# Attention and expert layer on one core: weighed sums in pairs, sums of squares from two fp32r halves, the key's projection in two steps, bounds read earlier

## Chip, cores, metric

One core of one Trainium2 chip. The metric is the device time of one execution in microseconds (us), the median of several runs.

## The reference, cut to what is computed

```python
# x: (4, 512, 512), context: (4, 512, 512), 32 heads of 16, D = 512
def xattn(x, context, Wq, Wk, Wv):
    q = x @ Wq.T; k_raw = context @ Wk.T; v_raw = context @ Wv.T
    q = q.reshape(b, n, 32, 16).transpose(0, 2, 1, 3)
    kv = jnp.concatenate([k_raw, v_raw], axis=-1).reshape(b, m, 32, 16, 2)
    k = kv[..., 0].transpose(0, 2, 1, 3); v = kv[..., 1].transpose(0, 2, 1, 3)
    q, k = rmsnorm(q), rmsnorm(k)            # over the 16 of a head
    attn = softmax(einsum('bhnd,bhmd->bhnm', q, k) * 16 ** -0.5)
    return einsum('bhnm,bhmd->bhnd', attn, v)...

x = x + xattn(layernorm(x), ctx, Wq, Wk, Wv)
# then a layer of 7 routed experts (top 2 of 7) and one shared expert, each
#   u = t @ Wup + bup;  g = silu(u @ Wgate + bgate) * u;  y = g @ Wdown + bdown
x = x + ffn(layernorm(x))
```

## The kernel before

The kernel has two phases. **Attention** takes the first 452 us or so. It runs over 16 units: unit u is one batch b of four and one group g of four, a group being 128 of the 512 columns, that is 8 heads. Each unit has eight steps s; a step is one half of the heads (`ab`, s // 4) against 128 of the 512 keys (`mt`, s % 4). "Step 6" below always means s = 6 of a unit. Projections are made two units ahead: while unit u is in its steps, TensorE makes the queries of unit u + 2 into PSUM bank `bank_b` (`q_turns`) and its keys into `bank_a` (`k_turns`). One such projection is 12 matmuls of 128x128 by 512 columns, called turns. Everything there is fp32 split in a high and a low fp32r part, three products for one.

What each engine does for a step, in its own program order (each engine waits on semaphores; nothing else sets the order):

- TensorE: `scored(u, s)` writes the scores into the PSUM tile `scores` (8 matmuls on 32 rows each). There is one such tile, so it waits until the exponential of the step before has been taken. Then `between(u, s)`: some turns, sums, transposes. Then `weighed(t - 1)`: the probabilities of the step before by the values (`o_ps`, 4 fp32 matmuls on 17 columns each, recorded as 8). Then `after(u, s)`.
- ScalarE: `before_exp(u, s)`, a small operation or two (squares, logarithm, root, copy of `o_ps`), then the exponential of `scores` into `probs`, of which there are two.
- VectorE: `step(u, s)`, a list of normalisations, splits and copies out of PSUM.
- GpSimd: two squarings of roots for each unit, and now and then a layer norm (`norm2`).

The sum over each head's 16 squares for the rms norm goes like this: ScalarE squares the projection out of its bank into the SBUF tile `sq`, TensorE multiplies `sq` by a matrix of ones in blocks (`blocks`) in plain fp32 into the PSUM tile `tr` (`sum_q`, `sum_k`), VectorE takes `tr` (`sums_q`, `sums_k`), ScalarE takes the root. `tr` is used in turn by many things, in a fixed order, the transposes of the outputs (`out_transposes`, L708) and the routing (`gate_parts`, `gates`, `norm2_transposes`) among them. In unit u, `square_q(u + 2)` stands ahead of the exponential of step 6 and `sum_q(u + 2)` in step 7; `square_k(u + 1)` stands ahead of that of step 2 and `sum_k(u + 1)` in step 2.

Units are not alike. With g = 1 of the first three batches VectorE also splits the next batch's input in step 6 (`x_low`, `x_split`), with g = 2 it splits the next context in steps 1 to 3 (`context_split`), and with g = 2 and g = 3 of the first three batches TensorE makes the next values too (`v_all`, 12 matmuls in step 2 and 12 in step 5). For the last two units nothing is projected.

**Experts** take the rest: the shared expert on 8 tiles of 256 rows (`tile(0)` to `tile(7)`), then the routed experts on tiles whose number is only known at run time. During tiles 2 to 6 the routing is worked out: `starts` gives where each expert's tiles begin, `table_out` which rows stand in which slot. From it GpSimd gathers the rows of the first routed tile (`gather(NA)`), which TensorE transposes within tile 7. The engines read the expert bounds into registers (`bound`).

Of the kernel before, what the change touches and what calls it, by code (L numbers as in the profile page):

```python
# [15 lines left out]
def moe_layer(nc, x, x_t, ctx_t, wq_t, wk_t, wv_t, w_all, b_up_gate, b_down, w_router, b_router, gate_bias, xn_dram,  # L16
# [20 lines left out]
    with ExitStack() as ctx:  # L37
# [46 lines left out]
        probs = asb("probs", [P, 2, QUADS, SEQ])  # L84
# [95 lines left out]
        K_TURNS = {6: (0, 4), 7: (4, 5), 0: (5, 9), 1: (9, 12)}  # L180
        Q_TURNS = {3: (0, 5), 4: (5, 9), 5: (9, 12)}
# [142 lines left out]
        def _(pool):  # L324
# [8 lines left out]
            def root(n, half):  # L333
# [11 lines left out]
                                    pattern=[[HD, P // HD], [0, HD]], channel_multiplier=-1).then_inc(blocks_set, 1)  # L345
            nc.gpsimd.memset(v_sb[0][:, :, :, HD:], 1.0).then_inc(ones_set, 1)
# [50 lines left out]
            def gather(n):  # L397

                first = isinstance(n, int) and n == NA
                if first:  # L400
                    pool.wait_ge(xl_done, n * 2)
                    pool.wait_ge(table_ready, 1)
                    pool.wait_ge(dense_stored, 16)
# [201 lines left out]
        def _(pe):  # L605
# [8 lines left out]
            def scored(u, s):  # L614
# [16 lines left out]
            def weighed(t):  # L631
# [149 lines left out]
            def between(u, s):  # L781
# [1237 lines left out]
```

## Time and profile before

| | |
|---|---|
| median of 3 runs | 966.19 us (966.05 to 966.67) |
| the profiled execution, time | 966.36 us |
| the profiled execution, span | 964.6 us |
| TensorE busy | 944.2 us (98%) |
| VectorE busy | 706.1 us (73%) |
| ScalarE busy | 497.4 us (52%) |
| GpSimd busy | 208.1 us (22%) |

The span is what the trace covers. The time is that of the same execution as the runs are timed, 1.8 us above its span. Busy time of TensorE counts an operation until its modelled end, so that two short waits between overlapping operations hardly show in it.

### The profile page before, as it was taken

How to read it: one execution, taken by the hardware profiler on the slowest of the kernel's cores; microseconds unless marked ns; L12 is line 12 of the kernel's file. 1: busy time of each engine (PE TensorE's matmuls, PEld its weight loads, DVE VectorE, ACT ScalarE, POOL GpSimd, SP SyncE). 2: the span in 40 equal slices, each digit the busy share in tenths (PEclk: the TensorE clock that was granted, in tenths of full speed). 3: DMA queues.
4: the chain of work that ended last, by engine and by line, in shares of the span. 5: the costliest groups of instructions: out<-in, count | busy, mean ns of one | idle time of the engine just before them, and what ended most of it. 6: DMA issues, size and time to landing. Idle time of an engine off the chain costs nothing.

```text
span 964.6 us, 17835 instructions
## 1 busy us (share of the span) xinstructions
PE 944.2 (98%) x6676; PEld 681.4 (71%) x6676; DVE 706.1 (73%) x1459; ACT 497.4 (52%) x619; POOL 208.1 (22%) x225
## 2 busy tenths in 40 slices
PE   8999999999999999999999999999999999999995
PEld 7634444454444454345989999999999999999995
DVE  7798767886678757885978886865867686758654
ACT  4588668866787658887234313323424244324221
POOL 1011000311012200320300001423323323333331
PEclk9999999999999999999999999999999999999998
DMA  9400100100201110313523104834535536625422
GB/s 334 170 1 23 66 1 1 45 33 24 76 2 44 45 66 1 110 56 130 203 74 112 67 23 142 235 73 71 180 67 146 117 71 204 197 48 166 115 49 39
DMA packets 32512, 87.42 MB, mean 91 GB/s; under 512 B 7744, under 2 KB 7744, under 8 KB 28352
## 3 DMA queue, kind: packets, MB, share of 16 engines
q1 hardware_dynamic: 21920, 60.70, 17.9%
q0 software_dynamic: 10528, 25.87, 12.9%
q8 instruction: 40, 0.66, 0.3%
q14 instruction: 24, 0.20, 0.1%
HBM read 61.83 MB, written 24.72 MB: 90 GB/s over the span
## 4 chain that ended last, share of the span: by engine, by line
PE 87%; DVE 6%; issue 2%; ACT 2%; DMA 1%; DVEq 0%; POOLq 0%; POOL 0%; SPq 0%; ACTq 0%
PE z_ps L907 16%; PE y_ps L907 15%; PE u_ps L907 15%; PE o_ps L642 11%; PE scores L626 8%; PE bank_a L679 5%; PE bank_b L663 5%; PE bank_b L649 2%; PE xt_ps L921 2%; PE bank_a L649 2%; PE tr L708 1%; PE tr L702 1%; PE tr L697 1%; DMA ctx_raw<-ctx_t 1%; ACT probs L1180 1%
## 5 line engine op out<-in xcount | busy, mean ns | idle before, releaser
L1180 ACT ACTIVATE probs<-scores 128x2048 f32<-128x2048 f32 x128 | 240.5, 1879 | 64.1 <-PE scores L626 61.1
L907 PE MATMUL z_ps<-u_hi,w_sb 128*128 128x256 f32 x896 | 167.6, 285 | 0.8 <-DVE u_lo L1869 0.8
L907 PE MATMUL u_ps<-x_hi,w_sb 128*128 128x256 f32 x864 | 159.2, 283 | 0.0
L1210 ACT ACTIVATE u_hi<-u_ps,b_ug 128x256 fp32r<-128x256 f32 x108 | 45.3, 471 | 198.8 <-PE u_ps L907 198.8
L907 PEld LDWEIGHTS z_ps<-u_hi,w_sb 128*128 128x128 f32 x896 | 140.6, 190 | 2.1 <-DVE u_lo L1869 1.2
L907 PE MATMUL y_ps<-w_sb,g_hi 128*128 128x512 f32 x448 | 139.8, 393 | 0.2 <-DVE g_lo L1887 0.2
L907 PEld LDWEIGHTS u_ps<-x_hi,w_sb 128*128 128x128 f32 x864 | 135.7, 190 | 1.1
L642 PE MATMUL o_ps<-probs,v_sb 128*17 128x512 f32 x1024 | 134.7, 598 | 0.0
L907 PE MATMUL z_ps<-u_lo,w_sb 128*128 128x256 f32 x448 | 126.5, 282 | 0.0
L907 PE MATMUL u_ps<-x_lo,w_sb 128*128 128x256 f32 x432 | 122.2, 283 | 0.0
L1222 ACT ACTIVATE s_sb<-z_ps,b_ug 128x256 f32<-128x256 f32 x112 | 47.0, 471 | 99.6 <-PE z_ps L907 99.6
L626 PEld LDWEIGHTS scores<-q_st,k_hi 32*128 32x128 f32 x512 | 24.7, 182 | 104.0 <-ACT probs L1180 63.4
L427 POOL DMA_INDIRECT out<-y_sb,target x42 | 67.3, 1602 | 127.8 <-DVEq L1911 120.4
L907 PEld LDWEIGHTS y_ps<-w_sb,g_hi 128*128 128x128 f32 x448 | 82.3, 188 | 17.2 <-issue 0.8
L1869 DVE SCALAR_TENSOR_TENSOR u_lo<-u_ps,b_ug,u_hi 128x256 fp32r<-128x256 f32 x108 | 47.2, 478 | 64.0 <-ACT u_hi L1210 61.5
L907 PE MATMUL y_ps<-w_sb,g_lo 128*128 128x512 f32 x224 | 88.0, 393 | 0.0
L907 PEld LDWEIGHTS z_ps<-u_lo,w_sb 128*128 128x128 f32 x448 | 85.1, 190 | 0.0
L907 PEld LDWEIGHTS u_ps<-x_lo,w_sb 128*128 128x128 f32 x432 | 82.2, 190 | 1.1
L1882 DVE SCALAR_TENSOR_TENSOR g_sb<-u_ps,b_ug,s_sb 128x256 f32<-128x256 f32 x112 | 53.9, 481 | 30.3 <-ACT s_sb L1222 30.1
L626 PE MATMUL scores<-q_st,k_hi 32*128 32x512 f32 x512 | 64.7, 494 | 3.5 <-ACT probs L1180 1.9
L350 POOL TENSOR_TENSOR r<-r 128x512 f32<-128x512 f32 x16 | 17.4, 1088 | 189.5 <-ACT r L1067 189.5
L1190 ACT ACTIVATE w_sb<-w_raw 128x1024 fp32r<-128x1024 f32 x42 | 42.3, 1058 | 28.1 <-PE y_ps L907 28.1
(247 smaller groups left out, 1594.9 us busy)
## 6 DMA issues: line engine op xcount, KB each, us to landing
w_raw<-w_all SPq DMA_DIRECT2D x27, 1024.0 KB, 6.9
ctx_raw<-ctx_t SPq DMA_DIRECT2D x4, 1024.0 KB, 6.8
out<-x_sb SPq DMA_DIRECT2D x16, 256.0 KB, 2.0
xg<-xt_dram POOLq DMA_DIRECT2D x14, 256.0 KB, 3.4
x_sb<-x SPq DMA_DIRECT2D x1, 3072.0 KB, 17.4
xn<-x_t SPq DMA_DIRECT2D x12, 256.0 KB, 4.4
xn_dram<-xn SPq DMA_DIRECT2D x12, 256.0 KB, 2.1
xt_dram<-xt SPq DMA_DIRECT2D x6, 512.0 KB, 3.0
```

The costliest lines, as they stand in the source:

```text
L427: nc.gpsimd.indirect_dma_start(out=out, in_=y_sb[:, h, :], in_offset=None, compute_op=ALU.add, out_offset=bass.IndirectOffsetOnAxis(ap=tar ...
L626: last = nc.tensor.matmul(scores[:, j, :], part[rows, u % 2, ab, mt * P:(mt + 1) * P], q_st[rows, u % 2, ab, :], start=(part is k_hi), sto ...
L642: last = nc.tensor.matmul(o_ps[32 * j:32 * j + HD + 1, :], v_sb[b % 2][:, mt, head, :], probs[:, t % 2, j, :], start=(mt == 0), stop=(mt = ...
L663: last = nc.tensor.matmul(bank_b[:], (wq_hi, wq_lo)[a][:, g, c, :], (xt_hi, xt_lo)[b][:, c, :], start=(c == 0 and a + b == 0), stop=(c == ...
L679: last = nc.tensor.matmul(bank_a[:], (wk_hi, wk_lo)[a][:, g, c, :], (ctx_hi, ctx_lo)[b][:, c, :], start=(c == 0 and a + b == 0), stop=(c = ...
L907: ins = nc.tensor.matmul(out_ps, stat[a], mov[b], start=(first and a + b == 0), stop=(last and a == 1), skip_group_check=True)
L1180: nc.scalar.activation(probs[:, t % 2], scores[:], ACT.Exp).then_inc(p_ready, 1)
L1190: nc.scalar.activation(w_sb[par][:, m, 0, two], w_raw[:, m, two], ACT.Copy).then_inc(hi_done, 1)
L1210: last = nc.scalar.activation(u_hi[:, c, :], u_ps[:, b, a, :], ACT.Identity, bias=b_ug[:, par, 0, c:c + 1])
L1222: nc.scalar.activation(s_sb[:, c, :], z_ps[:, b, a, :], ACT.Silu, bias=b_ug[:, par, 1, c:c + 1]).then_inc(s_done, 1)
L1869: nc.vector.scalar_tensor_tensor(u_lo[:, c, :], u_ps[:, b, a, :], bias[:, c:c + 1], u_hi[:, c, :].bitcast(FP32), ALU.add, ALU.subtract)\
L1882: nc.vector.scalar_tensor_tensor(g_sb[:, c, :], u_ps[:, b, a, :], bias[:, c:c + 1], s_sb[:, c, :], ALU.add, ALU.mult).then_inc(g_done, 1)
```

## The change

- **Weighed sums.** `probs` has three buffers. In units 0 to 13 `weighed` comes straight behind `scored` (in steps 2 and 7 behind `between`), and by the table `SUMMED` in these steps: 0 (those of steps 6 and 7 of the unit before), 2 (step 0), 3 (steps 1 and 2), 4 (step 3), 6 (steps 4 and 5), none in 1, 5 and 7.
- **Squares.** For 20 of the sums (`HALVED`: the 14 `sum_q(u + 2)` and the `sum_k(u + 1)` of the six units with g of 2 or 3 in the first three batches) GpSimd copies `sq` into the fp32r tile `sq_hi` (`squares_high`), VectorE writes the rest `sq_lo` (`squares_low`), and TensorE sums the two in two fp32r matmuls in place of one fp32 matmul (`sum_halves`). VectorE's piece stands in step 6 behind `stack_k`, or in step 2.
- **Turns.** `k_turns(u + 2)` has 6 turns in step 7 and 6 in step 1 of the next unit, behind `sum_q`; it had 4, 1, 4 and 3 in steps 6, 7, 0 and 1. `q_turns` has 1, 5 and 6 turns in steps 3, 4 and 5; it had 5, 4 and 3.
- **Buffers.** `q_st`, `k_hi` and `k_lo` have one copy in place of two, so that their writers wait for `scored` of the unit before (`half_scored`).
- **Experts.** VectorE reads the bounds in pieces in tiles 4 to 7 ahead of the gate's products (`during_z`), not all at the end of tile 7. The first gather takes its rows straight from `table`, not from a copy in `index`, and GpSimd reads its bound ahead of it.

```diff
-        probs = asb("probs", [P, 2, QUADS, SEQ])
+        probs = asb("probs", [P, 3, QUADS, SEQ])
-        q_st = asb("q_st", [P, 2, 2, SEQ], FP32R)
-        k_hi, k_lo = (asb(n, [P, 2, 2, CTX], FP32R) for n in ("k_hi", "k_lo"))
+        q_st = asb("q_st", [P, 2, SEQ], FP32R)
+        k_hi, k_lo = (asb(n, [P, 2, CTX], FP32R) for n in ("k_hi", "k_lo"))
...
-        K_TURNS = {6: (0, 4), 7: (4, 5), 0: (5, 9), 1: (9, 12)}
-        Q_TURNS = {3: (0, 5), 4: (5, 9), 5: (9, 12)}
+        K_TURNS = {7: (0, 6), 0: (6, 6), 1: (6, 12)}
+        Q_TURNS = {3: (0, 1), 4: (1, 6), 5: (6, 12)}
+        SUMMED = {0: (-2, -1), 1: (), 2: (0,), 3: (1, 2), 4: (3,), 5: (), 6: (4, 5), 7: ()}
...
+            def squares_high(use):
+                pool.wait_ge(sqk_done if use[0] == "sum_k" else sqq_done, use[1] + 1)
+                for other, n in HALVED.items():
+                    if n == HALVED[use] - 1:
+                        pool.wait_ge(tr_ready, TR_AT[other] + 1)
+                nc.gpsimd.tensor_copy(sq_hi[:], sq[:]).then_inc(sq_high, 1)
...
+            def sum_halves():
+                nc.tensor.matmul(tr[:], blocks_r[:], sq_hi[:], start=True, stop=False)
+                nc.tensor.matmul(tr[:], blocks_r[:], sq_lo[:], start=False, stop=True).then_inc(tr_ready, 1)
+
             def sum_q(u):
                 begin("tr", TR_AT, ("sum_q", u), tr_free)
-                pe.wait_ge(sqq_done, u + 1)
-                nc.tensor.matmul(tr[:], blocks[:], sq[:], start=True, stop=True).then_inc(tr_ready, 1)
+                if ("sum_q", u) in HALVED:
+                    pe.wait_ge(sq_low, HALVED["sum_q", u] + 1)
+                    sum_halves()
...
                 elif s == 7:
                     if ahead:
+                        sum_q(u + 2)
                         k_turns(u + 2, *K_TURNS[s])
-                    if ahead:
-                        sum_q(u + 2)
...
             for u in range(UNITS):
                 for s in range(STEPS):
                     scored(u, s)
-                    between(u, s)
-                    if u or s:
-                        weighed(STEPS * u + s - 1)
+                    alone = u >= UNITS - 2
+                    if alone or s in (2, 7):
+                        between(u, s)
+                    for back in SUMMED[s] if not alone or (u, s) == (UNITS - 2, 0) else (s - 1,):
+                        if u or back >= 0:
+                            weighed(STEPS * u + back)
+                    if not alone and s not in (2, 7):
+                        between(u, s)
                     after(u, s)
...
+            def squares_low(use):
+                dve.wait_ge(sq_high, HALVED[use] + 1)
+                nc.vector.tensor_tensor(sq_lo[:], sq[:], sq_hi[:].bitcast(FP32), ALU.subtract).then_inc(sq_low, 1)
...
                     if nxt:
                         stack_k(u + 1, 0)
+                    if u + 2 < UNITS:
+                        squares_low(("sum_q", u + 2))
...
-            gather(NA)
             pool.wait_ge(start_ready, 1)
             total = bound(pool, ER)
+            gather(NA)
             gather(NA + 1)
...
-            tile(7, 0, x_tile=14, during_u=last_split, during_y=bounds)
+            tile(7, 0, x_tile=14, during_u=last_split, during_z=lambda: bounds(7, ER + 1))
```

How the change moves instructions, at the places that the prediction speaks of. TensorE of unit 8, step 7 and step 0 of unit 9 before (`bank_a` rows are turns of `k_turns`, the `sq,blocks` row is `sum_q(10)`):

```order
L626 MATMUL scores<-q_st,k_hi 128x512 x4
L626 MATMUL scores<-q_st,k_lo 128x512 x4
L679 MATMUL bank_a<-ctx_lo,wk_hi 128x512
L697 MATMUL tr<-sq,blocks 128x512
L642 MATMUL o_ps<-probs,v_sb 17x512 x4
L626 MATMUL scores<-q_st,k_hi 128x512 x4
L626 MATMUL scores<-q_st,k_lo 128x512 x4
L679 MATMUL bank_a<-ctx_hi,wk_lo 128x512
L679 MATMUL bank_a<-ctx_hi,wk_hi 128x512
L679 MATMUL bank_a<-ctx_lo,wk_hi 128x512
L679 MATMUL bank_a<-ctx_hi,wk_lo 128x512
L642 MATMUL o_ps<-probs,v_sb 17x512 x4
```

The same steps of TensorE now, from step 7 on:

```order
L660 MATMUL scores<-q_st,k_hi 128x512 x4
L660 MATMUL scores<-q_st,k_lo 128x512 x4
L729 MATMUL tr<-sq_hi,blocks_r 128x512
L730 MATMUL tr<-sq_lo,blocks_r 128x512
L713 MATMUL bank_a<-ctx_hi,wk_hi 128x512
L713 MATMUL bank_a<-ctx_lo,wk_hi 128x512
L713 MATMUL bank_a<-ctx_hi,wk_lo 128x512
L713 MATMUL bank_a<-ctx_hi,wk_hi 128x512
L713 MATMUL bank_a<-ctx_lo,wk_hi 128x512
L713 MATMUL bank_a<-ctx_hi,wk_lo 128x512
L660 MATMUL scores<-q_st,k_hi 128x512 x4
L660 MATMUL scores<-q_st,k_lo 128x512 x4
```

The sum stands first behind the scores of step 7, with six turns behind it and no weighed sum in that step.

VectorE of unit 5 (g = 1) now, from the transposes' copy of step 5 (`rec`, `o_n`, `x_sb` are `finalize`) to `sums_q` of step 7 (`ssq`):

```order
L1512 RECIPROCAL rec<-tr 128x16
L1513 TENSOR_TENSOR o_n<-tr,rec 128x256
L1518 TENSOR_TENSOR x_sb<-x_sb,o_n 128x4x4x16
L1394 TENSOR_TENSOR xt_lo<-xn,xt_hi 128x512
L1400 CAST xt_hi<-xn 128x512
L1401 TENSOR_TENSOR xt_lo<-xn,xt_hi 128x512
L1501 STREAM_SHUFFLE twin<-kn 128x512
L1504 TENSOR_SCALAR k_hi<-twin,sign 128x512
L1505 SCALAR_TENSOR_TENSOR k_lo<-twin,sign,k_hi 128x512
L1441 TENSOR_TENSOR sq_lo<-sq,sq_hi 128x512
L1445 TENSOR_TENSOR ssq<-tr,eps 128x512
```

The row `sq_lo` is new, ahead of `ssq`; the others stand as before. In units with g = 0 the three rows of `xt_lo` and `xt_hi` are missing.

GpSimd around the first gather, before:

```order
L407 COPY index<-table 128x2
L411 DMA xg<-xn_dram,index 128x520 x2
L293 TENSOR_LOAD start_i
L293 ISA x2
L407 COPY index<-table 128x2
```

and now:

```order
L312 TENSOR_LOAD start_i
L312 ISA x2
L446 DMA xg<-xn_dram,table 128x520 x2
L441 COPY index<-table 128x2
L446 DMA xg<-xn_dram,index 128x520 x2
```

The copy ahead of the first gather is gone, and the read of the bound stands ahead of it.

## Rows read from the trace of the kernel before

**Rows 1.** The page: busy time by engine (part 1), costliest groups (part 5).
```profile
PE 944.2 (98%) x6676; PEld 681.4 (71%) x6676; DVE 706.1 (73%) x1459; ACT 497.4 (52%) x619; POOL 208.1 (22%) x225
...
L642 PE MATMUL o_ps<-probs,v_sb 128*17 128x512 f32 x1024 | 134.7, 598 | 0.0
```

**Rows 2.** TensorE's waits, 30 to 455 us: total, times, longest, in us.
```profile
PE scores L626 <- ACT probs L1180: 1.9, 4, 0.7
```

**Rows 3.** Timeline of unit 8 from step 5: start, duration, engine.
```profile
267.46 0.50 PE L626 MATMUL scores<-q_st,k_hi 32*128 32x512 f32 x4
...
268.92 0.60 PE L708 MATMUL tr<-ident,o_sb 128*128 128x128 f32 x4
...
270.03 0.59 ACT L1038 ACTIVATE sq<-bank_b 128x512 f32<-128x512 f32 x1
270.44 0.50 PE L626 MATMUL scores<-q_st,k_hi 32*128 32x512 f32 x4
...
272.23 1.05 PE L642 MATMUL o_ps<-probs,v_sb 128*17 128x512 f32 x8
...
272.94 0.68 DVE L1290 BATCH_NORM_STATS2 stats<-x_sb 128x6 f32<-128x512 f32 x1
273.21 0.51 PE L626 MATMUL scores<-q_st,k_hi 32*128 32x512 f32 x4
...
274.22 1.02 PE L697 MATMUL tr<-sq,blocks 128*128 128x512 f32 x2
...
276.16 0.50 PE L626 MATMUL scores<-q_st,k_hi 32*128 32x512 f32 x4
```

**Rows 4.** Timeline: starts of steps 2 and 3 of unit 9.
```profile
282.01 0.51 PE L626 MATMUL scores<-q_st,k_hi 32*128 32x512 f32 x4
...
284.73 0.50 PE L626 MATMUL scores<-q_st,k_hi 32*128 32x512 f32 x4
```

**Rows 5.** Timeline: step 5 of unit 9, VectorE's last piece ahead, unit 10.
```profile
290.51 0.50 PE L626 MATMUL scores<-q_st,k_hi 32*128 32x512 f32 x4
...
297.48 0.75 DVE L1438 SCALAR_TENSOR_TENSOR k_lo<-twin,sign,k_hi 128x512 fp32r<-128x512 f32 x1
...
299.23 0.51 PE L626 MATMUL scores<-q_st,k_hi 32*128 32x512 f32 x4
```

**Rows 6.** Timeline of unit 10 (g = 2), from the start of step 1 to step 3.
```profile
302.89 0.51 PE L626 MATMUL scores<-q_st,k_hi 32*128 32x512 f32 x4
...
304.23 1.10 POOL L350 TENSOR_TENSOR r<-r 128x512 f32<-128x512 f32 x1 [9.14 <-ACT r L1067]
...
304.47 1.41 DVE L1430 SCALAR_TENSOR_TENSOR q_st<-twin,lower,q_st 128x512 fp32r<-128x512 f32 x1
...
309.25 0.69 DVE L1321 TENSOR_TENSOR ctx_lo<-ctx_raw,ctx_hi 128x512 fp32r<-128x512 f32 x1
...
311.43 0.51 PE L626 MATMUL scores<-q_st,k_hi 32*128 32x512 f32 x4
```

**Rows 7.** Timeline: GpSimd's layer norm in unit 7.
```profile
222.60 2.35 POOL L366 TENSOR_SCALAR xn<-x_sb,mv,rsqrt 128x512 f32<-128x512 f32 x1 [12.10 <-PE tr L747]
```

**Rows 8.** Timeline: starts of units 11 and 12.
```profile
330.69 0.51 PE L626 MATMUL scores<-q_st,k_hi 32*128 32x512 f32 x4
...
361.66 0.51 PE L626 MATMUL scores<-q_st,k_hi 32*128 32x512 f32 x4
```

**Rows 9.** TensorE's waits, 560 to 680 us, in us.
```profile
PE xt_ps L921 <- DMA xg<-xn_dram,index: 0.7, 1, 0.7
PE z_ps L907 <- DVE u_lo L1869: 0.6, 1, 0.6
```

**Rows 10.** Timeline: GpSimd's first gather; VectorE's first copy of tile 7.
```profile
575.27 0.91 POOL L407 COPY index<-table 128x2 int32<-128x2 int32 x1 [22.89 <-DVE table L1858]
...
577.08 1.12 POOL L411 DMA_INDIRECT xg<-xn_dram,index  x1 [0.90 <-POOL index L407]
...
597.58 0.69 DVE L1903 TENSOR_TENSOR y_sb<-y_ps,bd 128x512 f32<-128x512 f32 x1 [4.21 <-issue]
```

More of the change, by code:

```diff
@@ L177, in moe_layer @@
         A_AT, B_AT, TR_AT = uses("a"), uses("b"), uses("tr")
-        K_TURNS = {6: (0, 4), 7: (4, 5), 0: (5, 9), 1: (9, 12)}
-        Q_TURNS = {3: (0, 5), 4: (5, 9), 5: (9, 12)}
+        SUMS = [("sum_k", 0), ("sum_q", 0), ("sum_q", 1)]
+        HALVED = {}
+        for u in range(UNITS):
+            _, g, more, _ = batch_of(u)
+            if u + 1 < UNITS:
+                SUMS.append(("sum_k", u + 1))
+                if more and g >= 2:
+                    HALVED[SUMS[-1]] = len(HALVED)
+            if u + 2 < UNITS:
+                SUMS.append(("sum_q", u + 2))
+                HALVED[SUMS[-1]] = len(HALVED)
+        K_TURNS = {7: (0, 6), 0: (6, 6), 1: (6, 12)}
+        Q_TURNS = {3: (0, 1), 4: (1, 6), 5: (6, 12)}
+        SUMMED = {0: (-2, -1), 1: (), 2: (0,), 3: (1, 2), 4: (3,), 5: (), 6: (4, 5), 7: ()}
         def tile_of(b, i):
@@ L382, in _ @@
                     norm2(b - 1, 2)
+                if u + 2 < UNITS:
+                    squares_high(("sum_q", u + 2))
+                if behind and g == 2:
                     norm2(b - 1, 3)
@@ L625, in scored @@
                         rows = slice(32 * j, 32 * j + 32)
-                        last = nc.tensor.matmul(scores[:, j, :], part[rows, u % 2, ab, mt * P:(mt + 1) * P],
-                                                q_st[rows, u % 2, ab, :], start=(part is k_hi), stop=(part is k_lo),
+                        last = nc.tensor.matmul(scores[:, j, :], part[rows, ab, mt * P:(mt + 1) * P],
+                                                q_st[rows, ab, :], start=(part is k_hi), stop=(part is k_lo),
                                                 skip_group_check=True)
@@ L1033, in x_high, with squares_taken @@
                 nc.scalar.activation(xt_hi[:, c, :], xn[:, c % 2 if b else c, :], ACT.Copy).then_inc(xt_high, 1)
+            def squares_taken(use):
+                ahead = SUMS[SUMS.index(use) - 1]
+                if ahead in HALVED:
+                    act.wait_ge(sq_low, HALVED[ahead] + 1)
+                else:
+                    act.wait_ge(tr_ready, TR_AT[ahead] + 1)
             def square_q(u):
                 act.wait_ge(b_ready, B_AT["q", u] + 1)
-                act.wait_ge(tr_ready, TR_AT["sum_k", max(u - 1, 0)] + 1 if u != 1 else TR_AT["sum_q", 0] + 1)
+                squares_taken(("sum_q", u))
                 nc.scalar.activation(sq[:], bank_b[:], ACT.Square).then_inc(sqq_done, 1)
@@ L1042, in square_k @@
                 if u:
-                    act.wait_ge(tr_ready, TR_AT["sum_q", u] + 1)
+                    squares_taken(("sum_k", u))
                 nc.scalar.activation(sq[:], bank_a[:], ACT.Square).then_inc(sqk_done, 1)
@@ L1561, in step @@
                         context_split(b + 1, 1)
+                    if ("sum_k", u + 1) in HALVED:
+                        squares_low(("sum_k", u + 1))
                     if u == 0:
@@ L1935, in _, with bounds @@
             tile(3, 0, x_tile=6, before_x=totals_out, during_z=probabilities, during_y=steps_of(prefixes_out, starts))
-            tile(4, 0, x_tile=8, during_u=positions, during_y=lambda: hot_rows(0))
-            tile(5, 0, x_tile=10, during_u=lambda: hot_cols(0),
+            start_at = [0]
+            def bounds(first, end):
+                dve.wait_ge(start_ready, 1)
+                for e in range(first, end):
+                    start_at.append(bound(dve, e))
+            tile(4, 0, x_tile=8, during_u=positions, during_z=lambda: bounds(1, 3), during_y=lambda: hot_rows(0))
+            tile(5, 0, x_tile=10, during_u=lambda: hot_cols(0), during_z=lambda: bounds(3, 5),
                  during_y=steps_of(lambda: table_out(0), lambda: hot_rows(1)))
```

66 lines of the change are left out of this document (39 added, 27 removed).

## Prediction

> **What bounds the kernel now.** The page comes first: TensorE is busy 98% of the span, the weighed sums alone 134.7 us [rows 1]. Then the waits of TensorE in attention: in all of it only 1.9 us for the exponential [rows 2]. So attention is bound by TensorE's program, and what counts is each step's length, from one start of `scored` to the next. The timeline of one unit gives it, with its parts. Step 7 of unit 8 puts one turn between `scored` and the sum, 1.01 us after the step's start; step 5 puts three there, 1.46 us. So a turn is 0.23 us. Step 6 has four turns and reaches its weighed sum after 1.79 us, one turn and one change of shape (0.11 us) more than step 5; `scored` is then 0.67 us. A weighed sum takes 0.98 us to the next step (272.23 to 273.21), the fp32 sum 0.96 us (274.22, a weighed sum and 276.16), the transposes of step 5 0.54 us [rows 3]. Below all this lies a floor: `scores` is one tile, so a step is never shorter than scores, exponential and hand-over. Step 2 of unit 9 shows it, 2.72 us [rows 4]. Step 6 of unit 8 at 2.77 us is hardly above.
>
> Two stretches outside attention wait: 0.7 us for the first gathered rows and 0.6 us for `u_lo` [rows 9].
>
> **The change on TensorE alone.** Two weighed sums in a row should cost 0.98 + 0.86 us: each of the two passes of one streams for 0.43 us, since the group's mean is 598 ns and the pair spans 1.05 us [rows 1, 3], and only the last has a drain behind it. Bounds for the second are 0.86 and 0.98; I take 0.86. The halved sum takes two turns, 0.46 for 0.96 us. With these, a unit with g = 0 goes: step 0 with two weighed sums 2.5, so the floor 2.72; step 1 waits for ScalarE, which copies `o_ps` and takes a root after the second weighed sum, 2.87 (an estimate; together with step 0 5.59 us, against 282.01 - 276.16 = 5.85 now [rows 3, 4]); step 2 the floor; step 3 0.67 + 1.84 + 0.44 = 2.95; step 4 0.67 + 0.98 + 1.36 = 3.01; step 5 0.67 + 1.48 + 0.54 = 2.69, so the floor; step 6 the floor; step 7 0.67 + 0.46 + 1.37 + changes 0.2 = 2.70, so the floor. Sum 22.43 us against 23.07 of unit 9 [rows 3, 5]. So where nothing is late, 0.6 us a unit is all that is left of the saving, since the floor takes the rest.
>
> **The sum is late.** `sum_q` now stands first in step 7 and needs GpSimd's copy and VectorE's rest. Everything in units counts from the start of step 5 (T5).
>
> - The transposes of step 5 now stand behind six turns: T5 + 0.67 + 1.48 = 2.15 us, not 1.46 [rows 3]. VectorE's program has `finalize`, `stack_k` and then `squares_low`. In unit 8 VectorE is through with `stack_k` 4.02 us after the transposes start (268.92 to 272.94), waiting for nothing but these [rows 3]. So `squares_low` begins at 6.17, takes 0.69 as a subtraction of this shape does [rows 6], and with 0.1 for the hand-over the sum starts at 6.96.
> - TensorE is there at T5 + 2.72 + 2.72 + 0.67 = 6.11. It waits 0.85 us with six turns and the next `scored` queued behind. From the sum to the next unit are eight turns and two changes, 2.03: T5 + 8.99, so steps 5 to 7 take 9.0 us where they took 8.70 [rows 3]. With the other steps the unit is 23.3, +0.2. Units 4, 8, 12 and 13: **+0.9**.
> - GpSimd's copy: the square is taken 0.41 us before step 6 [rows 3], so the copy runs from T5 + 3.2. The trace has no such copy. It costs nothing at the price of the nearest row, 1.10 [rows 6], done at 4.3; at 2.35, the layer norm's [rows 7], done at 5.6, still ahead of 6.17. I take 1.1.
> - g = 1 with input to split: VectorE starts `k_lo` 6.97 us after T5 and needs 0.7 more before it could go on [rows 5]. The transposes' later place adds 0.2. So `squares_low` begins at 7.85, the sum at 8.63, the next unit at T5 + 10.66, against 8.72 [rows 5]. The steps before give 0.1 back. Units 5 and 9: +1.9 each. Unit 1 has a first step that now waits less: +1.2. In unit 0 VectorE is held up by the weights' splits just as far: +2.0. Together **+6.9**.
> - g = 2: `sum_k` is halved too, and stands behind `v_even` in step 2. VectorE starts the `ctx_lo` ahead of it 6.36 us after the start of step 1 [rows 6]. The rows for the next batch's epsilon had a weighed sum behind them in step 0 and have none now, so that VectorE's chain from them falls 0.98 us later in step 1. `squares_low` begins at 6.36 + 0.63 + 0.98 = 7.97, or at 7.3 without the hold of 0.66 us on `q_st` (below). TensorE could sum at 2.72 + 0.67 + 0.98 + twelve turns with a change, 2.87 = 7.24. Steps 1 and 2 together come to 8.7 to 9.4; I take 9.0, against 8.54 [rows 6]. In steps 6 and 7 VectorE has `v_out`, `stack_k`, the new piece and `parts_out` ahead of the sum: a wait of some 0.6 us. Against this step 0 gains 0.2 and step 5 0.3, and step 4 loses 0.3. Unit 10, 31.46 us now [rows 5, 8], goes to 32.0; units 2, 6 and 10: **+1.4**.
> - g = 3: here the copies have room in step 2. Step 0 saves 0.5 to 0.7, step 1 0.35, step 2 0.4, step 5 0.3; step 4 loses 0.2 and the last two steps 0.1. Unit 11 goes from 30.97 [rows 8] to 29.6; units 3, 7 and 11: **-3.3**.
> - Unit 14 keeps its weighed sums single but has six turns in step 1 where it had three, with a change for 0.6 us less the floor's 0.05 in step 0: **+0.5**. The third buffer of `probs` and the single buffers of `q_st` and `k_hi` cost nothing: their writers come a step or more after the last reader.
>
> Attention: +0.9 + 6.9 + 1.4 - 3.3 + 0.5 = **+6.4 us**.
>
> **Experts.** The gather starts where the copy does now, at 575.27 and not at 577.08 [rows 10]: 1.8 us earlier against a wait of 0.7 [rows 9], which goes. VectorE stands 4.21 us before its first copy of tile 7 reading seven bounds [rows 10], 0.6 each; now two at most stand in a tile's z phase, ahead of products with about that much slack. Then `u_lo` is in time and 0.6 goes [rows 9]. **-1.3 us**; if the two reads delay a `g_lo`, -1.0.
>
> Sum: 966.36 us, the profiled execution, + 6.4 - 1.3 = 971.5; the median lies 0.2 below that execution, so **971.3 us**.
>
> **A lock between VectorE and GpSimd.** In unit 10 `q_st`, two SBUF inputs, takes 1.41 us where it starts 0.24 us into GpSimd's squaring of 1.10 us [rows 6]; the one of this form ahead of the sum in unit 9 takes 0.75 [rows 5]. So it seems to have stood until GpSimd was done. The new copy would run from T5 + 3.2 in units with g = 0, where VectorE's `x_sb` addition (two SBUF inputs) is due at 3.7: 0.5 us more in the chain to the sum. The same in g = 1 (0.4) and ahead of `sum_k` in g = 2 (0.3): about +4 us, and 975.5 us in all. The Trainium skill ("SBUF — State Buffer", section "SBUF: two separate sides") states it as a rule: such an operation and one of GpSimd that reads SBUF hold the shared port pair exclusively, and the second fully blocks. By that rule the answer is this rival's 975.5, without it 971.3. The trace agrees in unit 10.
>
> **Rivals.**
> 1. *The sum is late as worked out*, 971.3 us. For it: the program order and unit 8's chain, in which VectorE waits for nothing else. Own range 967 to 974. Chance 0.45.
> 2. *Late, and the lock too*: 975.5. Against it: a GpSimd copy may be shorter than 1.1 us. Chance 0.17.
> 3. *Gain and loss cancel*: the sum comes 0.3 us earlier at each of its 17 late places (14 in step 7, 3 in step 2), 971.3 - 5.1 = 966.2. For it: my chains rest on the old order. Chance 0.18.
> 4. *Faster: the sum is not late*. Then all waits go: 2.3 in unit 0, 2.2 in units 1, 5 and 9, 0.85 in four units, about 0.6 in the six with g of 2 and 3, and 1.1 in three steps 2: 19 us, and 952 us. It decides if VectorE reaches `squares_low` by T5 + 5.3; unit 8's row has it at 5.48 even with the old, earlier transposes (272.94 - 267.46). So only part of it can come: with half of it 962. Chance 0.20.
>
> **How the numbers follow.** The measurement tells 0.2%, 1.9 us, from no change. Below 964.3: rival 4 and a part of rival 3, 0.23. Within: most of rival 3 and the lower edge of rival 1, 0.17. Above 968.1: 0.60. The range is 962 to 977: it leaves out the better half of rival 4 and a lock that costs more than reckoned.
>
> **What would show it.** TensorE's waits would have `tr <- sq_lo` as by far the longest, 14 to 20 times, 15 to 20 us in total, the longest over 2 us in units 0, 1, 5 and 9. Step 7 of a g = 0 unit would be about 3.5 us, step 3 2.95 and step 0 2.72; two weighed sums 1.84 us to the next instruction. Both waits of rows 9 would be gone. The prediction is wrong if `sq_lo` waits are under 5 us in total, if step 3 is over 3.1 us (the second weighed sum drains), or if GpSimd's copy and not VectorE ends the wait.

## The result: 977.2 us, a little slower

| | before | after |
|---|---|---|
| median | 966.29 us (966.05 to 966.67, 4 runs) | 977.2 us (976.19 to 978.18, 4 runs) |
| profiled execution, time / span | 966.36 / 964.6 us | 976.19 / 974.4 us |
| start of step 7 of unit 15 (attention all but over) | 451.62 us | 463.43 us |
| mean granted TensorE clock | 0.996 | 0.991 |

The ratio is 1.0112, with a 95% interval of 1.0099 to 1.0125. So the kernel is slower, as forecast, but the time lies just above the forecast range. The spans differ by 9.8 us: attention takes 11.8 us more, and what comes after it 2.0 us less (974.4 - 463.43 = 510.97 against 512.98). The four runs of after lie in two pairs, 976.2 and 976.3 with a recorded mean clock of 0.991 and 0.990, and 978.1 and 978.2 with 0.989 both; the profile is of the first.

**The page after.** TensorE's busy time and the chain that ended last:

```profile
PE 932.4 (96%) x6676; PEld 690.0 (71%) x6676; DVE 719.5 (74%) x1479; ACT 495.7 (51%) x619; POOL 220.8 (23%) x245
PE 81%; DVE 10%; ACT 4%; issue 3%; POOLq 0%; POOL 0%; DVEq 0%; ACTq 0%
```

TensorE has less to do, 932.4 against 944.2 us, and still ends later; VectorE has a tenth of the chain. Its waits in attention, 30 to 470 us (us in total, times, longest), where before there were [rows 2], 1.1 us once for `q_st` and 0.5 us more:

```profile
PE tr L729 <- DVE sq_lo L1441: 15.3, 10, 2.8
PE scores L660 <- ACT probs L1236: 3.7, 9, 1.3
PE tr L729 <- DVE xn L1420: 2.1, 4, 0.5
PE bank_b L683 <- DVE qn L1457: 1.8, 3, 0.6
```

In the experts the waits of [rows 9] are both gone.

**A unit with g = 0.** The timeline of unit 8 from step 5, which answers to [rows 3]:

```profile
275.38 0.50 PE L660 MATMUL scores<-q_st,k_hi 32*128 32x512 f32 x4
...
277.55 0.60 PE L754 MATMUL tr<-ident,o_sb 128*128 128x128 f32 x4
...
278.60 0.61 POOL L385 CAST sq_hi<-sq 128x512 fp32r<-128x512 f32 x1 [4.87 <-ACT sq L1094]
...
280.82 0.51 PE L660 MATMUL scores<-q_st,k_hi 32*128 32x512 f32 x4
...
281.56 0.69 DVE L1441 TENSOR_TENSOR sq_lo<-sq,sq_hi 128x512 fp32r<-128x512 f32 x1
...
282.40 0.47 PE L729 MATMUL tr<-sq_hi,blocks_r 128*128 128x512 f32 x1 [0.83 <-DVE sq_lo L1441]
...
284.40 0.50 PE L660 MATMUL scores<-q_st,k_hi 32*128 32x512 f32 x4
```

`squares_low` starts 6.18 us after the step 5 it is counted from, the sum at 7.02, the next unit at 9.02. The forecast had 6.17, 6.96 and 8.99. GpSimd's copy takes 0.61 us, and is done 2.3 us before anyone needs it.

**A unit with g = 1.** The timeline of unit 9, steps 6 and 7 and the start of unit 10, which answers to [rows 5]:

```profile
298.33 4.82 POOL L395 TENSOR_SCALAR xn<-x_sb,mv,rsqrt 128x512 f32<-128x512 f32 x2
...
302.94 0.69 DVE L1394 TENSOR_TENSOR xt_lo<-xn,xt_hi 128x512 fp32r<-128x512 f32 x1
303.10 1.00 POOL L385 CAST sq_hi<-sq 128x512 fp32r<-128x512 f32 x1
303.55 0.83 DVE L1400 CAST xt_hi<-xn 128x512 fp32r<-128x512 f32 x1
304.23 0.50 PE L660 MATMUL scores<-q_st,k_hi 32*128 32x512 f32 x4 [0.19 <-ACT probs L1236]
...
306.98 0.68 DVE L1441 TENSOR_TENSOR sq_lo<-sq,sq_hi 128x512 fp32r<-128x512 f32 x1
307.81 0.47 PE L729 MATMUL tr<-sq_hi,blocks_r 128*128 128x512 f32 x1 [2.85 <-DVE sq_lo L1441]
...
309.31 0.63 PE L713 MATMUL bank_a<-ctx_lo,wk_hi 128*128 128x512 f32 x1
...
310.29 0.80 PE L660 MATMUL scores<-q_st,k_hi 32*128 32x512 f32 x4
```

Here two things stand that no term of the forecast had. While GpSimd copies, a CAST of VectorE takes 0.83 us, where the same one took 0.42 before the change. And some 1.4 us behind the end of the wait of 2.85 us TensorE turns slow: the first turns behind the sum take 0.39 us as ever, from 309.31 on they take 0.63, and `scored`'s first four matmuls 0.80 and not 0.50. The table of stretches around the four long waits (columns: us, busy time of PE, PEld, DVE, ACT, POOL with the number of instructions, granted clock, DMA share, GB/s) has unit 0's wait and slow stretch, unit 1's slow stretch, unit 5's wait and what follows it, and unit 9's wait with three stretches behind it:

```profile
60.00:62.50 2.50, 0.00 (x0) 0.00 (x0) 2.43 (x5) 1.88 (x1) 0.00 (x0) 1.00 0.00 0
63.40:66.90 3.50, 3.50 (x18) 1.75 (x20) 3.12 (x7) 0.81 (x2) 0.00 (x0) 0.51 0.03 7
90.70:94.20 3.50, 3.50 (x19) 1.11 (x21) 3.01 (x6) 1.91 (x2) 0.00 (x0) 0.51 0.00 0
195.30:198.10 2.80, 0.04 (x4) 0.00 (x0) 2.64 (x6) 1.88 (x1) 0.00 (x0) 1.00 0.57 179
198.10:202.00 3.90, 3.84 (x28) 2.09 (x32) 2.74 (x6) 1.66 (x2) 0.00 (x0) 1.00 0.02 4
304.90:307.80 2.90, 0.06 (x4) 0.02 (x1) 2.69 (x6) 1.88 (x1) 0.00 (x0) 1.00 0.55 171
307.80:309.20 1.40, 1.39 (x6) 1.19 (x7) 0.66 (x1) 0.00 (x0) 0.00 (x0) 1.00 0.00 0
309.20:312.60 3.40, 3.40 (x19) 1.19 (x22) 3.02 (x7) 1.66 (x2) 0.00 (x0) 0.50 0.02 5
312.60:314.90 2.30, 2.30 (x20) 1.07 (x12) 0.03 (x1) 1.76 (x3) 0.00 (x0) 1.00 0.00 0
```

The granted clock has two levels, 1.2 and 2.4 GHz, so that 0.50 is the lower one throughout. It is down for 3.4 us each time, from 0.9 to 1.5 us after TensorE is back at work: behind the waits of unit 0 (2.57 us), unit 1 (2.70) and unit 9 (2.85). Behind that of unit 5, 2.82 us, it isn't down at all. The Trainium skill ("TensorE: Matmul & The Clock Gate", section "Part 1: The HAM clock gate (the "warmup" mystery)") says that the array's clock is halved after a stretch without work and comes back after sustained work; the rows agree for units 0, 1 and 9, and unit 5 shows that a stand of the same length doesn't always bring it.

### The profile page after: what moved, and what is told of

Its sections match the earlier page's. It is cut to its first block, busy times and chain, and to the rows that moved or that the text cites. A ratio compares the mean times of both kernels' runs of the same rounds, so it can differ in the third digit from the quotient of the medians.

```text
span 974.4 us, 17952 instructions
## 1 busy us (share of the span) xinstructions
PE 932.4 (96%) x6676; PEld 690.0 (71%) x6676; DVE 719.5 (74%) x1479; ACT 495.7 (51%) x619; POOL 220.8 (23%) x245
## 4 chain that ended last, share of the span: by engine, by line
PE 81%; DVE 10%; ACT 4%; issue 3%; POOLq 0%; POOL 0%; DVEq 0%; ACTq 0%
PE y_ps L955 16%; PE z_ps L955 16%; PE u_ps L955 16%; PE o_ps L676 8%; PE scores L660 6%; PE bank_b L697 4%; ACT probs L1236 3%; PE bank_a L713 3%; PE bank_b L683 2%; PE xt_ps L969 2%; PE bank_a L683 2%; DVE twin L1501 1%; PE tr L748 1%; DVE k_lo L1505 1%; DVE sq_lo L1441 1%
## 5 line engine op out<-in xcount | busy, mean ns | idle before, releaser
L676 PE MATMUL o_ps<-probs,v_sb 128*17 128x512 f32 x1024 | 127.9, 601 | 0.0
L676 PEld LDWEIGHTS o_ps<-probs,v_sb 128*17 128x17 f32 x1024 | 21.7, 97 | 60.0 <-issue 59.0
```

## The experiments

All but e4 start from the changed kernel. Times are medians, with the ratio to before and its interval.

**e1: all sums whole again, in fp32.** All else as changed (pairs of weighed sums, turns, experts):

```diff
+        HALVED = {}
-                if u + 2 < UNITS:
+                if ("sum_q", u + 2) in HALVED:
                     squares_high(("sum_q", u + 2))
```
(the same condition ahead of `squares_low` in VectorE's step 6)

> The changed kernel with all sums of squares in one fp32 matmul straight from sq again; pairs, turns, buffers and the experts' part stay. Theory A (the halves are late and TensorE stands for them, and loses its clock behind the longest of these stands): no wait for sq_lo is left, step 7 of a unit with g = 0 is about 3.2 us and not 3.57, that of units 1, 5 and 9 3.2 and not 5.6 to 6.1, the granted clock is 1.00 throughout attention; some 14 us less than the changed kernel, 962 to 964 us. Rival B (the pairs and the turns' new places are what costs): it stays near 976 us.

Measured: **960.37 us**, ratio 0.9937 (0.9921 to 0.9954). The time is 2 us below the range of theory A, and rival B falls. The waits for `sq_lo` are gone, and step 7 is 3.11 us in all units with g of 0 and 1. So the split of the squares alone turns a gain of 6 us into a loss of 11. Without it nearly every kind of unit is shorter than before: 22.9 against 23.07 (g = 0, unit 8), 31.03 against 31.46 (unit 10), 29.50 against 30.97 (unit 11).

**e2: the low half first.** `squares_low` is VectorE's first piece of step 6, ahead of the splits and `stack_k`:

```diff
+                    if u + 2 < UNITS:
+                        squares_low(("sum_q", u + 2))
                     if nxt:
                         stack_k(u + 1, 0)
-                    if u + 2 < UNITS:
-                        squares_low(("sum_q", u + 2))
```

> The changed kernel with VectorE's squares_low of sum_q first in step 6, ahead of x_low and stack_k, and not behind them. Theory A (VectorE's queue is what makes the sum late): step 7 of a unit with g = 0 falls from 3.57 to 2.75 us, that of units 1, 5 and 9 to 2.8 to 3.0; with g of 2 and 3 behind a first batch parts_out still holds the bank tr, so that these keep 3.65; 957 to 959 us in all. Rival (GpSimd's copy is the late link): VectorE waits for sq_high instead and step 7 stays over 3.3 us, above 970 us.

Measured: **963.92 us**, ratio 0.9973 (0.9963 to 0.9983), 5 to 7 us short of what was expected. In g = 0 it does what it should: unit 8 takes 22.61 us, step 7 2.82. In units 1, 5 and 9 step 7 still takes 3.60, 4.06 and 4.03 us. TensorE's waits:

```profile
PE scores L660 <- ACT probs L1236: 6.9, 13, 1.5
PE scores L660 <- DVE k_lo L1505: 3.4, 3, 1.3
...
PE tr L729 <- DVE sq_lo L1441: 0.6, 1, 0.6
```

and why, in unit 9:

```profile
289.36 4.82 POOL L395 TENSOR_SCALAR xn<-x_sb,mv,rsqrt 128x512 f32<-128x512 f32 x2
294.14 0.60 POOL L385 CAST sq_hi<-sq 128x512 fp32r<-128x512 f32 x1
294.85 0.69 DVE L1441 TENSOR_TENSOR sq_lo<-sq,sq_hi 128x512 fp32r<-128x512 f32 x1 [0.90 <-POOL sq_hi L385]
...
299.29 0.51 PE L660 MATMUL scores<-q_st,k_hi 32*128 32x512 f32 x4 [1.26 <-DVE k_lo L1505]
```

GpSimd's copy stands behind two layer norms in its own queue. VectorE now waits 0.90 us for it with the splits and `stack_k` queued behind, and 0.90 + 0.69 later it is `k_lo` that is late: `scored` of unit 10 waits 1.26 us. So in units 5 and 9 the rival's condition, VectorE waiting for `sq_high`, did hold. The wait moved from `tr` to `scores`. By these numbers VectorE has about 0.3 us of room there (0.90 + 0.69 - 1.26) for a piece of 0.69, so that `k_lo` would be late even without the wait for GpSimd; this is an estimate, the copy ahead of the layer norms was not tried. In unit 1, with no such wait, `scored` still waits 0.84 us for `k_lo`.

**e3: TensorE kept at work in the long waits.** Ten matmuls of 128 columns, whose result nobody reads, ahead of the sum in units 0, 1, 5 and 9:

```diff
                     if ahead:
+                        if u in (0, 1, 5, 9):
+                            pe.wait_ge(a_free, A_AT["k", u + 2])
+                            unread(bank_a[:, 0:P], 10)
                         sum_q(u + 2)
```

> The changed kernel with ten matmuls of 128x128 that nobody reads (some 2.3 us) in step 7 of units 0, 1, 5 and 9 ahead of the sum that TensorE waits for. They do no needed work and are done before the sum could start. If the drop of the granted clock behind these waits costs what I read from the steps behind them (scored at 1.15 and not 0.67 us), the clock is 1.00 there, steps 7 and 0 of these units lose 0.4 to 1.1 us each, and the time is some 4 to 6 us less than the changed kernel, 971 to 973 us. If the clock is not the reason for the slow steps, it is unchanged or some tenths slower.

Measured: **972.07 us**, ratio 1.0057 (1.0040 to 1.0074), 5.1 us below the changed kernel's median (4.1 by the spans of the two profiled executions), and the mean clock is 0.996 again. The stretches at and behind unit 9's sum now have the full clock:

```profile
305.00:307.40 2.40, 2.03 (x12) 1.45 (x12) 1.24 (x4) 0.40 (x1) 0.00 (x0) 1.00 0.00 1
307.40:312.00 4.60, 4.60 (x43) 2.23 (x43) 3.46 (x8) 3.44 (x5) 0.78 (x1) 1.00 0.00 0
```

The sums are no earlier. The gains stand in units 0 (32.71 to 31.79), 1 (26.19 to 25.32), 2 (31.64 to 30.55), 9 (25.89 to 25.41) and 10 (32.63 to 31.52), that is at and behind the sums of units 0, 1 and 9. Unit 5, where the changed kernel had kept its clock, stays as it was (25.39, 25.43), and unit 6 too: nothing but the held clock shows in the times. Steps 7 and 0 around each of the three slow stretches are together 1.4 to 1.5 us shorter.

**e4: the experts' part alone**, on the kernel before: the first gather reads `table` itself, and the bounds are read in tiles 4 to 7.

```diff
-                nc.gpsimd.tensor_copy(index[:], table[:, bass.ds((n - NA + 1) * 2, 2)]).then_inc(index_ready, 1)
+                    picked_rows = table[:, 2:4]
...
-            tile(7, 0, x_tile=14, during_u=last_split, during_y=bounds)
+            tile(7, 0, x_tile=14, during_u=last_split, during_z=lambda: bounds(7, ER + 1))
```

> The kernel before with the experts' part of the change alone (first gather from the table, bounds read in tiles 4 to 7). By the prediction 1.3 us less than before, 965.0; by the trace of the changed kernel, where the stretch behind attention is 2.0 us shorter, 964.3 us. Rival: the stretch is shorter there only because attention hands over in another state, and this one is within 0.3 us of before.

Measured: **964.24 us**, ratio 0.9977 (0.9967 to 0.9986), 2.2 us less. The first gather, and the transposes that waited for it:

```profile
575.66 1.18 POOL L412 DMA_INDIRECT xg<-xn_dram,table  x1 [23.49 <-DVE table L1857]
...
582.50 1.04 PE L920 MATMUL xt_ps<-ident,xg 128*128 128x128 f32 x8
```

In the kernel before the last matmul ahead of these transposes starts at 582.61 and they at 583.61, 1.00 us; now it is 0.12 (582.38 to 582.50). So the wait shown as 0.7 cost 0.88 from start to start. At the second place, at 604.46 us before, it is 0.82 for the 0.56 shown: against the kernel before, TensorE's groups start 0.23 us earlier ahead of the first place, 1.11 behind it, and 1.93 behind the second. The 0.23 comes from attention, where nothing was changed: step 0 of unit 11 takes 3.78 us in the profile of before and 3.54 here.

**e5: the turns ahead of the sum.** In step 7 the six turns of the key cover the wait:

```diff
-                        sum_q(u + 2)
                         k_turns(u + 2, *K_TURNS[s])
+                        sum_q(u + 2)
```

> The changed kernel with one edit: in step 7 the six turns of the key's projection stand ahead of the sum of the query's squares, not behind it. Theory (the wait for sq_lo is time that TensorE could fill, and the clock falls because it stands idle so long): the turns (6 at 0.23 us = 1.38) cover the wait. Step 7 of g = 0 units falls from 3.57 to about 2.74 (units 4, 8, 12, 13: -0.83 each = -3.3); in units 0, 1, 5, 9 sq_lo is done about 3.4 us into the step, turns end at 2.1, so about 1.4 us of wait is left of 2.85 (-1.5 each = -6) and the clock stays up (-5.1, as the run with fill showed); g = 2 and 3 lose 0.2 each of 6 (-1.2). Sum 961.6 us, 960 to 964. Rival (what follows from the sum, the root and the key's and query's norms, is itself just in time): the wait comes back in steps 0 to 2 as a wait for qn, kn or k_lo, and the time stays above 966. Second rival (the gap is not the sum's but the bank's: the turns wait too): 975 to 978.

Measured: **970.77 us**, ratio 1.0046 (1.0030 to 1.0063). That is 9 us too much for the theory. The rival (the wait comes back) has its time, above 966; the wait comes back for the most part at the exponential, and less at `qn`. Its waits:

```profile
PE scores L660 <- ACT probs L1236: 9.3, 15, 1.3
PE tr L729 <- DVE sq_lo L1441: 4.9, 4, 1.3
PE tr L793 <- DVEq L1446: 3.4, 4, 0.8
PE bank_b L683 <- DVE qn L1457: 3.3, 3, 1.1
```

Unit 8 falls to 22.60 us, step 7 to 2.82, and in units 0, 1, 5 and 9 the wait for `sq_lo` is 1.0 to 1.3 us and the clock stays up (mean 0.997), all as expected. But the second matmul of the sum now starts only 0.43 us before the next unit begins (279.68 and 280.11), and what hangs on it is late there. From the start of unit 9:

```profile
280.11 0.50 PE L660 MATMUL scores<-q_st,k_hi 32*128 32x512 f32 x4
280.18 0.69 DVE L1445 TENSOR_TENSOR ssq<-tr,eps 128x512 f32<-128x512 f32 x1 [0.64 <-PE tr L730]
...
281.06 0.63 ACT L1106 ACTIVATE r<-ssq 128x512 f32<-128x512 f32 x1 [1.10 <-DVEq L1447]
...
281.60 1.86 ACT L1236 ACTIVATE probs<-scores 128x2048 f32<-128x2048 f32 x1
...
283.51 0.51 PE L660 MATMUL scores<-q_st,k_hi 32*128 32x512 f32 x4 [0.82 <-ACT probs L1236]
```

ScalarE's small operation on `ssq` stands ahead of the exponential in its program. It comes at 281.06, so the exponential starts 1.49 us into the step and not 0.79, and step 0 takes 3.40 us for 2.72. With g of 2 and 3 the routing's transposes wait for the same bank (L793, 0.8 each), and in g = 2 `v_even` waits 0.5 us more for `qn`.

**e6 and e7: turns alone, pairs alone**, both on e1. In e6 every step has one weighed sum again:

```diff
-                    alone = u >= UNITS - 2
+                    alone = True
...
+                    for back in (s - 1,):
```

> The kernel of e1_fp32_sums with its weighed sums one a step again and the turns ahead of them, as before: only the two projections' turns stand as in the changed kernel (key 6 in step 7 and 6 in step 1, query 1, 5, 6 in steps 3 to 5). Theory (turns and pairs fit together, and neither is worth anything alone): steps 1, 5 and 7 hold six turns and a weighed sum and run over the floor of 2.72 us: by 0.23 a turn and 0.98 a weighed sum step 7 +1.2, step 5 +0.7, step 1 +0.6, step 4 +0.1, against -0.3 in step 3 and -0.1 in steps 0 and 6: +2.2 a unit over 14 units, so 990 to 997 us. Rival (the key's projection in two steps is what gains, by fewer changes of shape; pairs add nothing): 960 to 964.

Measured: **990.44 us**, ratio 1.0249 (1.0232 to 1.0266). In e7 the turns are those of before, and the calls in steps 6 and 7 too (not shown):

```diff
-        K_TURNS = {7: (0, 6), 0: (6, 6), 1: (6, 12)}
-        Q_TURNS = {3: (0, 1), 4: (1, 6), 5: (6, 12)}
+        K_TURNS = {6: (0, 4), 7: (4, 5), 0: (5, 9), 1: (9, 12)}
+        Q_TURNS = {3: (0, 5), 4: (5, 9), 5: (9, 12)}
```

> The kernel of e1_fp32_sums with the turns of before (key 4, 1, 4, 3 in steps 6, 7, 0, 1 and query 5, 4, 3 in steps 3 to 5): only the weighed sums stand two together, in steps 0, 3 and 6. Theory (as for e6_turns_only): steps 0, 3 and 6 hold two weighed sums (1.84) and four or five turns: 3.54, 3.77 and 3.54 against 2.78, 3.01 and 2.77, +2.3; steps 1, 5 and 7 fall to 2.72: -0.8. +1.5 a unit over 12 to 14 units: 979 to 985 us. Rival (a second weighed sum saves 0.12 wherever it stands, and that is the gain): 960 to 963.

Measured: **984.98 us**, ratio 1.0195 (1.0178 to 1.0212). Both lie within what the sums from single prices gave, e6 at its lower end and e7 at its upper, where steps 0, 3 and 6 each take 0.1 us more than reckoned. Steps 5, 6 and 7 of unit 8 take 3.68, 2.72 and 4.10 us in e6, and 2.72, 3.64 and 2.81 in e7, against 2.73, 2.72 and 3.11 with both parts. So neither part gains anything alone, and both rivals fall: six turns fill the steps that the pairs empty.

**e8: halves only where they are in time.** `sum_k` of g = 3 stays split, and `sum_q` of g = 0 with the low half first (units 4, 8 and 12); all else is whole:

```diff
-                if more and g >= 2:
+                if more and g == 3:
                     HALVED[SUMS[-1]] = len(HALVED)
             if u + 2 < UNITS:
                 SUMS.append(("sum_q", u + 2))
-                HALVED[SUMS[-1]] = len(HALVED)
+                if g == 0 and u:
+                    HALVED[SUMS[-1]] = len(HALVED)
```
(and `squares_low` ahead of `stack_k`, as in e2)

> The changed kernel with split squares only where the run with low half first showed them on time: sum_k in units 3, 7, 11 and sum_q in units 4, 8, 12 (there sq_lo is VectorE's first work of step 6); all other sums in fp32 as in e1_fp32_sums. Theory (a split sum is worth what its step has above the floor of 2.72 us, if it is on time): step 2 of units 3, 7, 11 5.45 to 5.06 (-0.39 x 3), step 7 of units 4, 8, 12 3.11 to 2.82 (-0.29 x 3): 960.4 - 2.0 = 958.4 us, 957.6 to 959.2. Rival (sq_lo still delays something behind it, as in units 1, 5, 9 of e2_low_first, where k_lo came 1.3 late): 960 to 962.

Measured: **958.62 us**, ratio 0.9921 (0.9904 to 0.9937), the best of all: 7.7 us below before. Step 7 of unit 8:

```profile
268.37 0.69 DVE L1442 TENSOR_TENSOR sq_lo<-sq,sq_hi 128x512 fp32r<-128x512 f32 x1
269.62 0.50 PE L661 MATMUL scores<-q_st,k_hi 32*128 32x512 f32 x4
...
270.29 0.50 PE L730 MATMUL tr<-sq_hi,blocks_r 128*128 128x512 f32 x1
...
272.44 0.51 PE L661 MATMUL scores<-q_st,k_hi 32*128 32x512 f32 x4
```

The low half is done at 269.06, before the step begins at 269.62. The sum follows `scored` at once, and the step takes 2.82 us, not 3.11. Step 2 of unit 11 takes 5.05, not 5.44 (e1). A split sum saves 0.3 to 0.4 us, then, where it isn't late.

**e9: no GpSimd copy in the g = 1 units.** On e3, VectorE makes the high half itself in units 0, 1, 5 and 9, right ahead of the low one:

```diff
             def squares_low(use):
+                if use in (("sum_q", 2), ("sum_q", 3), ("sum_q", 7), ("sum_q", 11)):
...
+                    nc.vector.tensor_copy(sq_hi[:], sq[:]).then_inc(sq_high, 1)
```

> The kernel of e3_fill with one edit: in units 0, 1, 5 and 9 the high half of the squares is copied by VectorE, right ahead of sq_lo, and not by GpSimd; VectorE has one more 128x512 operation in its queue there (the same CAST of xt_hi takes it 0.42 us). Theory (VectorE and GpSimd share a way to SBUF: in units 5 and 9 the CAST of xt_hi takes 0.83 us, not 0.42, while GpSimd copies, which then takes 0.92 and 0.97, not 0.61): without GpSimd's copy the CAST falls back to 0.42 in units 5 and 9 and pays for the new copy there; sum_q starts as late as in e3_fill, step 7 stays 5.58 to 5.60, and only units 0 and 1, where that CAST took 0.41 or does not stand, come 0.4 later: 972.1 + 0.8 = 972.9 us, 972.3 to 973.2. Rival (the 0.83 has another cause, the transfers of xn that land then): the CAST stays at 0.83 and each of the four sums comes 0.42 later: 973.8 us, 973.4 to 974.2.

Measured: **972.14 us**, ratio 1.0065 (1.0048 to 1.0081); e3 had 972.07 and 1.0057. The two were timed against different medians of before, 965.88 and 966.45, so against its own before e9 takes 0.6 us more, and by the spans of the profiled executions 0.1 (970.4 and 970.3); the theory had 0.8, and the intervals are wider than any of these. So the rows decide here, not the medians. In unit 9:

```profile
301.23 0.42 DVE L1406 CAST xt_hi<-xn 128x512 fp32r<-128x512 f32 x1
301.33 1.40 SPq L516 DMA_DIRECT2D xn<-x_t  x2
...
304.25 0.42 DVE L1451 CAST sq_hi<-sq 128x512 fp32r<-128x512 f32 x1
```

The CAST is at 0.42 although the transfer of `xn` still runs beside it, so the rival falls. Step 7 takes 5.66 and 5.65 us in units 5 and 9 against 5.60 and 5.58, and 5.51 and 5.65 in units 0 and 1 against 5.33 and 5.46, with one more VectorE operation of 0.42 in each chain. So the copy on GpSimd had cost VectorE nearly as much as its own copy in units 5 and 9, and more than half as much in units 0 and 1.

## Why the forecast was right in direction and too low

**Right: the sum is late, and where.** Waits for `sq_lo` were forecast as the longest, 14 to 20 times, 15 to 20 us. There are 15.3 us, but in 10 waits. In units 6, 7, 10 and 11 the wait ahead of the sum, 0.5 us each, is put down to `xn`, the read of `tr` by `parts_out`; and in step 2 of g = 2 it is `v_even` that waits, for `qn`, and not `sum_k`. In unit 8 each point of the chain is within 0.06 us. Step lengths of g = 0 (step 0 2.72, step 3 2.94, step 4 3.02, step 7 3.57) and the pair of weighed sums (1.85, from 270.09 to 271.94) are as worked out from single prices, and e6 and e7 show that these prices hold for other mixes to 0.1 us a step.

**The terms.** Units 4, 8, 12 and 13 cost 0.28 + 0.28 + 0.27 + 0.33 = 1.2, forecast 0.9. Units 3, 7 and 11 give 0.39 + 1.41 + 1.60 = 3.4, forecast 3.3 (0.2 of unit 11's is the long step 0 of before, see e4). Unit 14 costs 0.56, forecast 0.5. Units 0, 1, 5 and 9 cost 3.17 + 2.48 + 2.32 + 2.82 = 10.8, forecast 6.9. Units 2, 6 and 10 cost 1.57 + 0.02 + 1.17 = 2.8, forecast 1.4. The experts give 2.0 in the profiles and 2.2 in e4, forecast 1.3.

**The step that failed: the bullet on g = 1.** It let TensorE wait 2.5 us (8.63 - 6.11) and go on at its full clock as if nothing had been: the clock was a term put at nothing, without a reason. By e3 the lower clock behind these waits costs 4.1 us in the profiled execution and 5.1 by the medians. It lies in units 0, 1 and 9 and in the first steps of units 1, 2 and 10, which is also why the g = 2 term seems too small: unit 6, behind the wait that kept its clock, costs 0.02. With the clock held (e3) units 2, 6 and 10 cost 0.5 us together, 0.9 less than forecast, and units 0, 1, 5 and 9 8.6, 1.7 more. The forecast had the wait's length and didn't ask what TensorE does after so long a stand. With the clock held (e3, 972.1) the time is within a microsecond of the 971.3 forecast, but that is partly luck, because smaller errors cancel. Two of these:

- *The lock was a rival and should have been a term of about 2.4 us.* Beside the new copy one VectorE operation is longer in each of seven units: `kn` in unit 0 and `xt_lo` in unit 1 take 0.98 us and not 0.69, the CAST of `xt_hi` 0.83 and not 0.42 in units 5 and 9, and the first `ctx_lo` 1.04 and not 0.69 in units 2, 6 and 10. (`x_sb` in unit 3 takes 0.58 for 0.42, where nothing waits for it.) In e1, which has no copy, each has its usual time, and in units 0, 1, 5 and 9 in e9 too. All seven stand in the chain that TensorE then waits for. In units 0, 1, 5 and 9 that is 1.4 of the 1.7 us by which the forecast is too low with the clock held. In units 2, 6 and 10 it is 0.35 each, which returns in the wait of `v_even` for `qn`, 0.6 us and in e1 0.2. The row of unit 10, and the wait in e1:

```profile
318.26 1.04 DVE L1377 TENSOR_TENSOR ctx_lo<-ctx_raw,ctx_hi 128x512 fp32r<-128x512 f32 x1
PE bank_b L684 <- DVE qn L1458: 0.7, 3, 0.2
```

  But the rival's 4 us were too much: in g = 0 units the copy is all but over when VectorE's `x_sb` addition begins (it ends at 279.21, the addition starts at 279.12 and takes its usual 0.42), because it takes 0.61 us and not 1.1. The Trainium skill ("SBUF — State Buffer", section "SBUF: two separate sides") has the two shut each other out for a whole instruction. In unit 9 that fits roughly: the copy, started in VectorE's `xt_lo`, takes 1.00 us and not 0.61, and the CAST then ends 0.27 us behind it. It doesn't fit everywhere: the layer norms of GpSimd run from 298.33 to 303.15 by the record, and VectorE's addition of two SBUF inputs at 302.48 takes its usual 0.42.
- *The experts' term read the idle time, not the distance from start to start.* A matmul's recorded end lies behind the point at which the next could start, so the waits of 0.7 and 0.6 cost 0.88 and 0.82 (e4): 0.4 of the 0.7 us missing in the profiles. For the other 0.3 no place was found.

**Rival 4, the only one that would have ended faster**, failed as argued: VectorE reached `squares_low` at T5 + 6.18. Its premise wasn't had by order alone in all units: e2 has it with g = 0 (step 7 of unit 8 2.82 us) and ends at 963.9, near the 962 that the forecast gave for half of this rival, but moves the wait to `k_lo` with g = 1; e5 puts the sum last and moves it to the exponential.

What stays open is why unit 5's stand of 2.8 us kept the clock. The recorded clocks suggest that in the runs of 978.1 and 978.2 us it didn't, or that some other stand took it: one slow stretch more, 3.4 us at half clock, takes 0.0017 off the mean and by e3 costs 1.4 to 1.5 us, against 0.989 for 0.990 and 0.991 and 1.9 us. Nothing was kept of those runs that shows the place.

## What to carry over

When a wait is longer than any that the trace of before has on TensorE (1.1 us within attention here), its length is only the first part of its price: read the granted clock behind long stands, and count what the next steps cost at the lower level; ten matmuls that nobody reads gave back 5.1 us here. An operation that is split to unload a bound engine hands work to others, so check for every kind of unit, and not for the mean, that those have room ahead of the point of use: the split sum saves 0.3 to 0.4 us in six units (e8) and costs 2.2 to 3.1 in four others with the clock's part (units 0, 1, 5 and 9, against e1), and choosing by unit (e8) beats both kernels. A rearrangement of two parts that fill each other's holes has to be priced as a whole, by step: here the turns alone (e6) end 24 us above before, the pairs alone (e7) 19 above, and both together (e1) 6 below, the 2 us of the experts' part counted in all three.

## Not expected of the hardware

- The clock of TensorE fell to its lower level 0.9 to 1.5 us after stands of 2.57, 2.70 and 2.85 us in units 0, 1 and 9, for 3.4 us each, and did not after one of 2.82 us in unit 5 of the same execution. Stands of 1.0 to 1.3 us (e5) and one of 1.55 us (e2) never brought it down.
- A GpSimd copy of 128x512 with rounding takes 0.61 us in 16 of its 20 places, and 0.84 to 1.00 in units 0, 1, 5 and 9, where VectorE is in an operation of two SBUF inputs as it starts; a VectorE CAST behind it takes 0.83 us instead of 0.42, an operation of two SBUF inputs 0.98 instead of 0.69. To VectorE such a copy on GpSimd is then hardly cheaper than its own (e9).
